# Layer-norm statistics moved ahead of the softmax blocks, one denominator round in place of two, and an earlier context remainder, in a fused attention and feed-forward kernel

## What is computed

```python
# 1  attention of 1024 positions over 1024 positions; q, k from the context, v from x
x = x + einsum('bts,bsc->bct', softmax(q @ k), Wv @ layernorm(x) + bv)
# 2  feed-forward with the signs of the weights, scaled by an 8-way router
x = x + (xf * in_scale) @ sign(weight).T * out_scale + bias
# 3  cross attention of 128 rows over the block's 128 context rows
x = x + softmax(scores * scale) @ ctx
# 4  eight routed low-rank products
x = x + 2 * sum_h scores_h * (xf @ A_h.T) @ B_h.T
```

## Time and profile before

| what | value |
|---|---|
| median of 3 runs | 2138.33 us |
| the profiled execution | 2136.73 us |
| its span (first to last instruction) | 2134.9 us |
| TensorE, matmuls | 2096.1 us busy, 98% |
| VectorE | 1846.7 us busy, 87% |
| ScalarE | 1205.1 us busy, 56% |
| GpSimd | 263.5 us busy, 12% |
| the chain that ended last | TensorE 79%, VectorE 12%, issue 2%, ScalarE 1% |

### The profile page before, as it was taken

The page is one execution under the profiler, slowest core; times in us unless marked ns, Lnnn a source line. Parts: engine busy times, 40 slices in busy tenths (PEclk is TensorE's granted clock), DMA queues, the critical chain, the costliest instruction groups (busy, mean ns, idle before and its releaser), DMA issues.

```text
span 2134.9 us, 37999 instructions
## 1 busy us (share of the span) xinstructions
PE 2096.1 (98%) x12825; PEld 1735.5 (81%) x12825; DVE 1846.7 (87%) x3065; ACT 1205.1 (56%) x1817; POOL 263.5 (12%) x306
## 2 busy tenths in 40 slices
PE   9989999999999999999999999999999999999998
PEld 7867888888888888888888888888888888888786
DVE  8258899888889898888999888889898888999885
ACT  4145666655556666555566655556666555566642
POOL 0000111011111111111111011111111111111101
PEclk9999999999999999999999999999999999999999
DMA  6764343344534334453433445344343445333320
GB/s 215 217 197 149 119 135 117 115 157 139 175 108 149 124 108 149 138 167 125 156 117 104 136 138 167 128 157 129 113 126 133 157 128 171 124 131 115 110 70 31
DMA packets 161155, 290.53 MB, mean 136 GB/s; under 512 B 14208, under 2 KB 62608, under 8 KB 161104
## 3 DMA queue, kind: packets, MB, share of 16 engines
q1 hardware_dynamic: 161104, 289.87, 42.1%
HBM read 223.75 MB, written 25.17 MB: 117 GB/s over the span
## 4 chain that ended last, share of the span: by engine, by line
PE 79%; DVE 12%; issue 2%; ACT 1%; DVEq 0%; POOL 0%; POOLq 0%; ACTq 0%
PE acc L1349 11%; PE shared L1269 6%; PE acc L1310 6%; PE scores L1289 6%; PE acc L1311 6%; PE shared L1323 6%; PE acc L1312 6%; PE shared L1324 6%; DVE p_lo L1128 5%; PE scores L1338 4%; PE scores L1337 4%; DVE p_sum L1136 3%; PE scores L1275 3%; PE shared L1551 3%; PE scores L1526 2%
## 5 line engine op out<-in xcount | busy, mean ns | idle before, releaser
L1128 DVE TENSOR_TENSOR p_lo<-prob,p_hi 128x1024 fp32r<-128x1024 f32 x256 | 312.4, 1220 | 95.2 <-ACT p_hi L885 87.0
L878 ACT ACTIVATE prob<-scores 128x1024 f32<-128x1024 f32 x256 | 260.6, 1018 | 198.8 <-PE scores L1338 134.2
L989 DVE TENSOR_REDUCE neg_max<-scores 128x1 f32<-128x1024 f32 x256 | 307.0, 1220 | 43.0 <-PE scores L1289 41.4
L764 POOL TENSOR_TENSOR rstd<-var_eps,minus_half 128x1 f32<-128x1 f32 x128 | 126.2, 986 | 1720.0 <-DVE var_eps L979 1720.0
L1310 PE MATMUL acc<-cT_hi,m_ring 128*128 128x256 f32 x1024 | 303.0, 296 | 1.0 <-DVE x L1029 1.0
L1311 PE MATMUL acc<-cT_lo,m_ring 128*128 128x256 f32 x1024 | 288.5, 282 | 0.0
L1312 PE MATMUL acc<-cT_hi,m_ring 128*128 128x256 f32 x1024 | 288.3, 282 | 0.0
L885 ACT ACTIVATE p_hi<-prob 128x1024 fp32r<-128x1024 f32 x256 | 271.3, 1060 | 29.4 <-PE acc L1349 23.2
L1323 PE MATMUL shared<-signT,y_hi 128*128 128x512 f32 x512 | 205.3, 401 | 1.0 <-DVE y_lo L1035 1.0
L1337 PE MATMUL scores<-q_hl,k_hh 128*128 128x512 f32 x512 | 201.2, 393 | 1.9 <-DVE q_m L1110 1.5
L1310 PEld LDWEIGHTS acc<-cT_hi,m_ring 128*128 128x128 f32 x1024 | 195.5, 191 | 8.5 <-DVE x L1029 1.1
(11 more groups left out here) (254 smaller groups left out, 4212.0 us busy)
## 6 DMA issues: line engine op xcount, KB each, us to landing
m_ring<-m_units SPq DMA_DIRECT2D x512, 256.0 KB, 3.3
xn<-in_x SPq DMA_DIRECT2D x32, 512.0 KB, 4.1
x<-in_x SPq DMA_DIRECT2D x32, 512.0 KB, 5.1
c_val<-in_ctx SPq DMA_DIRECT2D x32, 512.0 KB, 4.0
out_x<-oscale SPq DMA_DIRECT2D x32, 512.0 KB, 3.0
c_in<-in_ctx SPq DMA_DIRECT2D x31, 512.0 KB, 3.2
c_odd<-in_ctx SPq DMA_DIRECT2D x16, 512.0 KB, 4.3
q_m<-q_hl SPq DMA_DIRECT2D x32, 256.0 KB, 3.1
```

The costliest lines, as they stand in the source:

```text
L989: nc.vector.tensor_reduce(neg_max[:, t:t + 1], scores[t % 2][:, :], AX_X, ALU.max, negate=True).then_inc(row_max, 1)
L1128: nc.vector.tensor_tensor(p_lo[s % 2][:, :], prob[s % 2][:, :], p_hi[s % 2][:, :].bitcast(F32), ALU.subtract).then_inc(p_lo_ready, 1)
```

## The change

`x[b]` gets memory of its own, `xn_main`, and SyncE loads it near the start of the round. Its statistics are made by VectorE behind the row maxima, ahead of the loop over `s`; GpSimd then serves norm 0 before norm 2; ScalarE applies the norm at s = 2 instead of s = 6. VectorE adds the eighth block into `p_sum` at s = 7, ahead of its `p_lo`, and TensorE makes one round of four denominator products in place of two. `c_lo` moves from s = 6 to s = 5. The four `neg_mean` become columns of one tile.

```diff
@@ memory
+        xn_main = sb("xn_main", [P, D])
...
-        neg_mean = [sb(f"neg_mean{i}", [P, 1]) for i in range(4)]
+        neg_means = sb("neg_means", [P, 4])
+        neg_mean = [neg_means[:, i:i + 1] for i in range(4)]
@@ SyncE, behind the key units 12 to 15
+                    if prepare and attend:
+                        sp.wait_ge(v_done, nth(2, b - 1, 2))
+                        sp.dma_start(xn_main[:, :], x[b]).then_inc(xn_loaded, 16)
...
-                        sp.wait_ge(v_done, nth(2, b - 1, 2))
-                        sp.dma_start(xn[:, :], x[b]).then_inc(xn_loaded, 16)
@@ GpSimd
-                    if chain:
-                        norm_scale(2, c)
                     if prepare:
                         norm_scale(0, b)
+                    if chain:
+                        norm_scale(2, c)
@@ ScalarE, in the loop over s
-                            act.wait_ge(p_summed, nth(6, a, (0, 0, 1)[s] if s < 3 else s - 2))
+                            act.wait_ge(p_summed, nth(7, a, (0, 0, 1)[s] if s < 3 else s - 2))
...
-                        if prepare and attend and s == 6:
-                            normalize(0, b, xn, xn)
+                        if prepare and attend and s == 2:
+                            normalize(0, b, xn_main, xn_main)
@@ VectorE
+                    if prepare:
+                        dve.wait_ge(xn_loaded, nth(16, b, 16))
+                        dve_prepare.begin(b)
+                        statistics(dve_prepare, 0, b, xn_main if attend else xn)
+                        dve_prepare.end()
                     for s in range(T):
+                        if attend and s == T - 1:
+                            dve.wait_ge(exp_ready, nth(8, a, T))
+                            dve.wait_ge(p_summed, nth(7, a, T - 2))
+                            nc.vector.tensor_tensor(p_sum[:, :], p_sum[:, :], prob[1][:, :], ALU.add).then_inc(p_summed, 1)
...
-                        if prepare and s == 3:
-                            dve.wait_ge(xn_loaded, nth(16, b, 16))
-                            dve_prepare.begin(b)
-                            statistics(dve_prepare, 0, b, xn)
-                            dve_prepare.end()
...
-                        if prepare and attend and s == 6:
+                        if prepare and attend and s == 5:
                             dve.wait_ge(c_hi_ready, nth(1, b, 0))
                             dve.wait_ge(scores_done, nth(8, a, 8))
@@ TensorE, at s = 7
-                            pe.wait_ge(p_summed, nth(6, a, 6))
+                            pe.wait_ge(p_summed, nth(7, a, 7))
                             pe.wait_ge(exp_ready, nth(8, a, 8))
-                            for p, first in ((p_sum, True), (prob[1], False)):
-                                for g in range(4):
-                                    last = mm(scores[1][32 * g:32 * g + 32, 0:2 * P], ones[:, :], p[:, g * 2 * P:(g + 1) * 2 * P],
-                                              start=first, stop=not first, tile_position=(0, 32 * g))
+                            for g in range(4):
+                                last = mm(scores[1][32 * g:32 * g + 32, 0:2 * P], ones[:, :], p_sum[:, g * 2 * P:(g + 1) * 2 * P],
+                                          start=True, stop=True, tile_position=(0, 32 * g))
```

More of the change, by code:

```diff
@@ L773, in body @@
                         nc.gpsimd.tensor_tensor(res[:, :], x1[:, :], bias_rows[:, :], ALU.add).then_inc(biased, 1)
+                    if prepare:
+                        norm_scale(0, b)
                     if chain:
                         norm_scale(2, c)
-                    if prepare:
-                        norm_scale(0, b)
                     if prepare and not attend:
@@ L919, in body @@
                     if prepare and not attend:
-                        normalize(0, b, xn, xn)
+                        normalize(0, b, xn_main, xn)
                     if prepare and not attend:
@@ L1134, in body @@
                             if 2 <= s < T - 1:
-                                dve.wait_ge(p_summed, nth(6, a, s - 1))
+                                dve.wait_ge(p_summed, nth(7, a, s - 1))
                                 nc.vector.tensor_tensor(p_sum[:, :], p_sum[:, :], prob[s % 2][:, :], ALU.add).then_inc(p_summed, 1)
@@ L1274, in values @@
                     for t in range(4 * h, 4 * h + 4):
-                        last = mm(scores[1][:, t * P:(t + 1) * P], xn[:, t * P:(t + 1) * P], wvT[:, :], start=True, stop=True)
+                        last = mm(scores[1][:, t * P:(t + 1) * P], xn_main[:, t * P:(t + 1) * P], wvT[:, :], start=True, stop=True)
                     last.then_inc(v_done, 1)
```

## The result

The changed kernel takes **2156.03 us** (median of 3 runs, 2155.81 to 2156.09) against 2138.33 (2137.7 to 2138.94): a ratio of 1.0086, interval 1.0072 to 1.01, 17.7 us slower. The forecast was 2156.0. The granted clock was 0.998 in all three runs. The profiled executions stand a little farther apart: spans of 2154.0 and 2134.9 us, 19.1 us.

A forecast was written before the change was run, and what follows sets the result against it. TensorE sets the pace, waiting for VectorE at W6 each round. VectorE's tail 0.52 plus step 3's norm 0.08 gives 0.60 us a round, +18.0 us over 30 rounds: median 2156 us, range 2143 to 2167.

The forecast's parts named there:

- The row maximum as the place where the freed time stops: VectorE's row maximum waits for TensorE's last score product, so only 0.24 of the freed 1.69 us is left.
- the rival on the other side: Freed time reaches W6, which does not move; 0.45 us a round gained, 2124 us; chance 0.09.
- the cover ahead of the loop: VectorE's 2.68 us idle before the first p_lo hides the moved statistics; 1 us of it stays.
- W6: TensorE's start of weigh_values at s = 6, waiting for VectorE's p_lo; forecast 0.89 us later in round 15.
- The second floor: c_lo at s = 5 waits for the last key scores, making the p_lo of s = 6 at least 0.74 us later.
- The denominator round: TensorE makes one round instead of two, saving 0.45 us; the way out to the transposes stays.
- one round of 0.45: Sign of a right forecast: in the changed profile the denominators take one round of 0.45 us.
- VectorE behind W6: VectorE's way through the added p_sum: p_lo of s = 7 0.72 us later, copy of the denominators 0.52.
- step 3's norm: ScalarE's norm, delayed by the one moved to s = 2, holds TensorE's transposes; 0.08 us a round, between 0 and 0.20.
- delay and saved round cancelling: Rival: the delay at W6 and the saved denominator round cancel; 2134 to 2142 us, chance 0.06.
- VectorE as the bound of the whole: Rival: VectorE takes on 1.135 us in 32 rounds, 36 us, giving 2175 us; chance 0.02.
- the remainder's step: Making c_lo at s = 5 puts it ahead of the p_lo of s = 6; W6 comes 0.89 us later.

The follow-up runs named there:

- c: Changed kernel with the remainder c_lo back at s = 6, two denominator rounds and no added sum: 2133.06 us, ratio 0.998.
- e: Changed kernel with c_lo in the memory of y_lo, made at s = 4, and the norm of x[b] at s = 7: 2125.93 us, ratio 0.9945.
- h: Changed kernel with c_lo in the memory of y_lo, made at s = 4, the norm staying at s = 2: 2131.11 us, ratio 0.9971.
- a: Changed kernel with only the remainder c_lo moved back from s = 5 to s = 6: 2158.79 us, ratio 1.0102.
- d: Kernel before the change with one denominator round and the added p_sum, nothing else: 2161.76 us, ratio 1.0116.
- f: Changed kernel with two denominator rounds and no added sum, c_lo staying at s = 5: 2166.81 us, ratio 1.0134.
- g: Changed kernel with the added sum on GpSimd instead of VectorE, c_lo at s = 6, norm at s = 7: 2179.31 us, ratio 1.0193.

## Why the prediction was right

- **The row maximum as the place where the freed time stops: right.** It idles 0.77 us, as in round 32, and starts 0.43 behind the mark where 0.42 was forecast. The statistics with their memory and the norm at s = 2 (c) gained 3.8 us of the 51 that 1.69 in each of 30 rounds would be. This is why the rival on the other side, 2124, did not come. Of the cover ahead of the loop 0.68 us stayed, where 1 us was expected.
- **W6: right.** 0.90 later where 0.89 was worked out, with the remainder directly ahead of that `p_lo`. The second floor did not enter.
- **The denominator round: right.** From W6 to the transposes it is 5.23 us instead of 5.67, 0.44 saved where the step put 0.45. The one round took 0.57 with its way out to the transposes, as the second of the two had (0.55); half of the pair was not what was saved. (The sign "one round of 0.45" names what was saved; what stays is the 0.57.) The transposes came 0.46 later (forecast 0.44).
- **VectorE behind W6: right in mechanism, a little too small.** The added sum started 0.29 behind `r_inv`, not 0.20, so that `p_lo` of s = 7 came 0.81 later and not 0.72, the copy of the denominators 0.62 and not 0.52, and the turned denominators 0.60. This way, and not W6, is the later one, as the text took it (0.52 against 0.44), and the chain of the changed kernel goes through it.
- **The remainder of the sum.** 0.66 a round was measured for 0.60 in the text (62.28 us for 62.1); 0.06 of it lies behind the turned denominators, where 0.08 was put for step 3's norm. Between e and h the norm's place, at s = 7 and s = 2, is worth 0.12 to 0.17, inside the bounds of 0 to 0.20 that were given for s = 6 and s = 2. The 30 rounds came to 19.8 us for 18.0. The start, put at 0, gained 1.16 us, more than half of it in a part whose time differs between executions; this took back part of what the larger round cost. That the median came out within 0.1 us is luck: the total is nearer than its terms. Against the profiled execution of before 2154.7 were forecast, and 2155.81 were measured.
- **Of the rivals**, delay and saved round cancelling (2134 to 2142) did not come: the 0.90 at W6 still stood as 0.46 at the transposes. VectorE as the bound of the whole (2175) did not come: in the changed round TensorE is busy for 60.97 of 62.34 us and VectorE for 57.02. W6 is the one place in the kernel before, as the text says, but with the added sum it is not: run a shows a second one, for `res`, nearly as late; it is VectorE's unbroken way behind the row maximum that decides, not its share of the span.
- **Whether the parts were judged as a whole.** The text priced the remainder's step as a loss of 0.89. In this kernel undoing it gains nothing: with the added sum there, the remainder costs no less at s = 6 (a; the two intervals overlap), since VectorE's work from the row maximum to the inverse denominators is the same in either order. Ahead of the row maximum the remainder costs 24.2 us less (h).

## What to carry to other kernels

Price an added instruction by the stretch between two waits in which it lies, not by its engine's idle share: VectorE had 5.9 us idle in a round, but between the row maximum and the inverse denominators so little that a sum of 1.13 us made these 0.83 later (d). Time freed ahead of a wait for another engine is lost at that wait, unless independent work is put into the gap; here that work was the remainder, and memory of its own is what allowed the move (e). Where two waits lie close together, undoing one edit at a time shows neither (a, f): look for the edit that relieves both.

## What the runs showed of the hardware

A sum of two SBUF operands on GpSimd blocks one on VectorE: 3.13 us instead of 1.22 for VectorE's, with nearly all its work done after GpSimd's 3.06 us were over (g). The 3.13 us are the rest of GpSimd's instruction, 2.04 us from 1046.73 to 1048.77, and 1.09 of its own. The one that started first kept its time: VectorE's remainder, already running, took its 1.22, and GpSimd's sum behind it 3.06 where it took 2.36 with VectorE idle at its start (round 32). The Trainium skill says under "SBUF — State Buffer", Who interferes with whom, that the port pair which the two engines share is an exclusive lock, and that a VectorE instruction with two SBUF inputs contends with a GpSimd instruction that reads SBUF. Run g agrees with these numbers. GpSimd, busy for 12% of the span, is therefore no free place for such a sum beside VectorE's own.
